# Attention output kept in columns: denominators beside every output row instead of transposes on TensorE

## The reference

```
Q, K, V = x @ Wq.T + bq, ctx @ Wk.T + bk, ctx @ Wv.T + bv      # split into 16 heads of 16
attn    = softmax(Q K^T / 4)                                   # (8, 16, 112, 375)
context = (attn V) joined back to (8, 112, 256)
y       = context @ W_o.T + b_o + x
out     = (y - mean(y)) / sqrt(var(y) + 1e-5) * gamma + beta
```

## Time and profile before

| | us |
|---|---|
| median of 3 runs | 141.18 |
| lowest, highest | 141.05, 143.31 |
| profiled execution | 142.0 |
| its span | 140.1 |
| TensorE busy | 129.5 (92%) |
| VectorE busy | 96.6 (69%) |
| ScalarE busy | 90.1 (64%) |
| GpSimd busy | 81.9 (58%) |

### The profile page before, as it was taken

One profiled execution on the slowest core, in us unless ns is written; L12 is line 12 of the kernel. 1 busy time (PEld: TensorE's weight loads), 2 busy tenths in 40 slices (PEclk: granted clock), 3 DMA queues, 4 the chain that ended last, 5 costly groups with the idle time before them and its releaser, 6 DMA issues.

```text
span 140.1 us, 3936 instructions
## 1 busy us (share of the span) xinstructions
PE 129.5 (92%) x1477; PEld 113.6 (81%) x1477; DVE 96.6 (69%) x225; ACT 90.1 (64%) x187; POOL 81.9 (58%) x105
## 2 busy tenths in 40 slices
PE   4999997699999999998999999999999999999960
PEld 4799965589788979797989998999899888878720
DVE  5987799787837883668559756975697787521442
ACT  0887545358476857767684959575957758788620
POOL 8358899991722852205279866850589007498271
PEclk9999999999999999999999999999999999999997
DMA  4997794875189942642235026732270100011102
GB/s 146 317 347 255 231 296 129 297 238 187 54 185 285 272 126 70 218 135 98 68 120 215 5 72 188 256 120 72 90 276 0 25 19 5 8 36 33 37 0 66
DMA packets 16099, 19.59 MB, mean 140 GB/s; under 512 B 2624, under 2 KB 15488, under 8 KB 16080
## 3 DMA queue, kind: packets, MB, share of 16 engines
q1 hardware_dynamic: 14960, 17.42, 38.4%
q0 software_dynamic: 640, 1.64, 4.8%
q10 hardware_dynamic: 480, 0.28, 0.7%
HBM read 6.30 MB, written 0.92 MB: 52 GB/s over the span
## 4 chain that ended last, share of the span: by engine, by line
PE 73%; SPq 9%; DVE 7%; DMA 5%; issue 3%; ACTq 1%; ACT 1%; POOLq 0%; DVEq 0%
PE m_bank L881 16%; PE pv_bank L993 14%; PE st_bank L975 14%; PE mx_bank L942 13%; PE m_bank L1025 4%; SPq L326 4%; SPq L266 4%; DMA q_stack<-shift_half 3%; PE m_bank L1004 2%; PE mx_bank L975 2%; DMA q_stack<-shift 2%; DVE k_stack L725 2%; DVE mx L748 2%; PE m_bank L902 1%; PE m_bank L1012 1%
## 5 line engine op out<-in xcount | busy, mean ns | idle before, releaser
L748 DVE TENSOR_REDUCE mx<-mx_bank 112x1 f32<-112x375 f32 x128 | 63.7, 541 | 22.3 <-PE mx_bank L942 21.9
L633 ACT ACTIVATE pw<-st_bank 125x448 f32<-125x448 f32 x86 | 45.1, 546 | 18.1 <-PE st_bank L975 17.8
L942 PE MATMUL mx_bank<-k_stack,q_stack 128*112 128x376 f32 x128 | 43.3, 352 | 0.2
L975 PE MATMUL st_bank<-q_stack,k_stack 128*125 128x224 f32 x172 | 34.9, 284 | 2.3 <-DMA q_stack<-shift_half 1.8
L975 PEld LDWEIGHTS st_bank<-q_stack,k_stack 128*125 128x125 f32 x172 | 28.5, 186 | 6.1 <-issue 3.6
L942 PEld LDWEIGHTS mx_bank<-k_stack,q_stack 128*112 128x112 f32 x128 | 22.0, 176 | 3.4 <-DVE mx L748 1.7
L430 POOL TENSOR_TENSOR k_hl<-k_full,k_hl 128x376 fp32r<-128x376 f32 x10 | 10.0, 1001 | 20.2 <-ACT k_hl L549 20.2
L993 PE MATMUL pv_bank<-pw,v_sb 125*17 125x112 f32 x744 | 21.5, 260 | 0.0
L993 PEld LDWEIGHTS pv_bank<-pw,v_sb 125*17 125x17 f32 x744 | 16.7, 97 | 3.1 <-issue 1.9
L881 PE MATMUL m_bank<-w_hl,c_hl 128*125 128x256 f32 x126 | 18.2, 282 | 0.0
L404 POOL TENSOR_TENSOR c_hl<-c_raw,c_hl 128x752 fp32r<-128x752 f32 x6 | 11.1, 1854 | 10.5 <-ACT c_hl L520 10.5
(11 more groups left out here) (113 smaller groups left out, 177.1 us busy)
## 6 DMA issues: line engine op xcount, KB each, us to landing
k_stack<-k_hl SPq DMA_DIRECT2D x48, 188.0 KB, 2.7
c_raw<-ctxT SPq DMA_DIRECT2D x7, 375.0 KB, 3.8
q_stack<-q_hl SPq DMA_DIRECT2D x9, 112.0 KB, 2.2
x_space<-x_nat SPq DMA_DIRECT2D x4, 224.0 KB, 3.2
out<-yo SPq DMA_DIRECT2D x8, 112.0 KB, 2.0
pw<-wT SPq DMA_DIRECT2D x2, 256.0 KB, 4.2
q_stack<-q_hl POOLq DMA_DIRECT2D x3, 168.0 KB, 2.8
q_stack<-q_hl SPq DMA_DIRECT2D x3, 168.0 KB, 2.8
```

The lines of the kernel that those rows point to most:

```text
L633: nc.scalar.activation(p_tile[0:KC, n % PR, :, :], st_of(n)[0:KC, 0:4 * Q].rearrange("p (j q) -> p j q", j=4), ACT.Exp, scale=float(DK) ** ...
L748: nc.vector.tensor_reduce(mx[b % 2][:, h % 2, q_pair(h // 2):q_pair(h // 2) + 1], mx_bank[n % MR][0:Q, 0:KV], axis=AX_X, op=ALU.max, negat ...
L942: nc.tensor.matmul(mx_bank[n % MR][0:Q, 0:KVP], q_stack[k][:, side, q_pair(h // 2), b - Q_STACKS[k][0], :], k_stack[b % 3][:, h // 2, :], ...
L975: last = nc.tensor.matmul(st_of(n)[0:KC, k * 2 * Q:(k + 1) * 2 * Q], k_stack[i % 3][:, 2 * g + k, c * KC:(c + 1) * KC], q_stack[qk][:, :, ...
```

## The change

V gets 32 columns a head instead of 17: between its 16 columns stand 16 of ones (`VW = 2 * DK`, `v_sb` is `[..., DK, 2]`). The product with the exponentials then has an output row and a row of its denominators in turn, on all 128 partitions. `wo` and the bias of V are put in the order of these rows on the host (`by_output`).

For batches 0 to 6 the transposes of the raw and of the scaled output are gone. ScalarE copies the bank three times: to `o_raw`, its first groups of each pair to `o_normT`, the second to `den` (for batch 6 VectorE does it). Two transfers then put the odd rows of `o_normT` and the even rows of `den` in place. VectorE inverts `den` whole, GpSimd multiplies and adds the bias in two halves. OUT and the layer norm run two batches behind instead of three, and for batch 6 in the last batch.

```diff
-VW = DK + 1
+VW = 2 * DK
-U_OUT, U_OT, U_Q, U_CONTEXT = 0, 6, 11, 5
+U_OUT, U_LN, U_Q, U_CONTEXT, U_NORM = 5, 7, 11, 5, 8
-NORM_WITH = {3: 0, 4: 1, 5: 2, 6: 3, 7: 5}
-U_MT = (8, 7, 6, 6, 6, 6, 5)
+U_MT = (8, 7, 7, 7, 7, 7, 4)
+OUT_AT = {i: U_OUT for i in range(2, B - 2)} | {B - 2: 8, B - 1: 5}
+NORM_AT = {i: U_LN for i in range(2, B - 2)} | {B - 2: 8, B - 1: 5}
...
+            def swap_rows(b):
+                sp.wait_ge(o_raw_ready, b + 1)
+                raw = o_raw[b % 2][:, :].rearrange("p (e s q) -> p e s q", e=EC, s=2)
+                sp.dma_start(den[0:PART - 1:2, :, :], raw[1:PART:2, :, 0, :]).then_inc(swap_in[b % 2], 16)
+                sp.dma_start(o_normT[b % 2][1:PART:2, :, :], raw[0:PART - 1:2, :, 1, :]).then_inc(swap_in[b % 2], 16)
...   # SyncE, in each batch i >= 1, after K's transfers and ahead of the next context and shift
+                if i >= 1:
+                    swap_rows(i - 1)
...   # GpSimd
+            nc.gpsimd.memset(v_sb[2][:, :, :, :, :], 1.0).then_inc(v_ones[2], 1)
+            def scale_output(b):
+                pool.wait_ge(rden_ready, b + 1)
+                nc.gpsimd.tensor_tensor(o_normT[b % 2][:, :, :], o_normT[b % 2][:, :, :], den[:, :, :],
+                                        op=ALU.mult).then_inc(o_scaled, 1)
+                pool.wait_ge(o_scaled, b + 1)
+                pool.wait_ge(bv_in, 16)
+                for e in range(EC):
+                    last = nc.gpsimd.tensor_scalar(o_normT[b % 2][:, e, :], o_normT[b % 2][:, e, :], bv[:, e:e + 1], None,
+                                                   op0=ALU.add)
+                last.then_inc(o_normT_ready, 1)
...
                 if i + AHEAD < B:
-                    for t in range(2):
-                        subtract_k(i + AHEAD, t)
+                    subtract_k(i + AHEAD, 0)
+                if i >= 1:
+                    scale_output(i - 1)
+                if i + AHEAD < B:
+                    subtract_k(i + AHEAD, 1)
...
             for b in range(B - V_AHEAD - 3, B - 1):
                 inverse_deviation(b)
                 scale_rows(b)
+                if b + 2 < B - 1:
+                    scale_output(b + 2)
             inverse_deviation(B - 1)
...   # ScalarE, units 1 and 2 of batches 1 to 6
+            nc.scalar.copy(v_sb[1][:, :, :, :, 1], v_sb[0][:, :, :, :, 1]).then_inc(v_ones[1], 1)
+            def take_raw(b):
+                act.wait_ge(pv_done, NG * (b + 1))
+                if b >= 2:
+                    act.wait_ge(swap_in[b % 2], 32 * (b // 2))
+                nc.scalar.copy(o_raw[b % 2][:, :], pv_bank[:, 0:NG * Q])
+            def take_o(b):
+                src = pv_bank[:, 0:NG * Q].rearrange("p (e s q) -> p e s q", e=EC, s=2)
+                if b >= 2:
+                    wait_full(act, "OUT", b - 2)
+                nc.scalar.copy(o_normT[b % 2][:, :, :], src[:, :, 0, :])
+                if b >= 1:
+                    act.wait_ge(o_scaled, b)
+                nc.scalar.copy(den[:, :, :], src[:, :, 1, :]).then_inc(o_raw_ready, 1)
-            def take_o_norm_t(b, *job):
...   # VectorE: units 2 and 4 of batch 7 for batch 6, unit 8 else
-            nc.vector.memset(v_sb[0][:, :, :, :], 1.0).then_inc(v_ones, 1)
-            nc.vector.memset(pv_bank[:, :], 0.0).then_inc(pv_clear, 1)
+            nc.vector.memset(v_sb[0][:, 0, :, :, :], 1.0).then_inc(warm_ready, 1)
+            nc.vector.memset(v_sb[0][:, 1:NC, :, :, :], 1.0).then_inc(v_ones[0], 1)
-            def normalise(b):
+            def take_o_last():
+                b = B - 2
...   # the same three copies on VectorE
+            def invert(b):
+                dve.wait_ge(swap_in[b % 2], 32 * (b // 2 + 1))
+                nc.vector.reciprocal(den[:, :, :], den[:, :, :]).then_inc(rden_ready, 1)
...   # TensorE
-            def transpose_o(b):
-            def norm_columns(dst, b):
-            def transpose_o_norm(b):
                     for h in heads[:1]:
                         scores_for_max(h)
+                    if i + 1 < B and u == U_MT[i]:
+                        transpose_max(i + 1)
+                    if i >= 2 and u == OUT_AT[i]:
+                        out_project(i - 2)
...
```

More of the change, by code:

```diff
@@ L72 @@
 for _i in range(1, B - V_AHEAD):
-    if _i >= 3:
-        M1_JOBS.append(("OUT", _i - 3))
     M0_JOBS.append(("V", _i + V_AHEAD, 0))
     M1_JOBS.append(("V", _i + V_AHEAD, 1))
-    M0_JOBS.append(("MT", _i + 1))
-    M1_JOBS.append(("OT", _i - 1))
+    if _i >= 2:
+        M0_JOBS.append(("OUT", _i - 2))
+    M1_JOBS.append(("MT", _i + 1))
     if _i + AHEAD < B:
@@ L128, in build @@
                 .rearrange("p (s e n) -> p s e n", s=2, e=EC))
-        v_sb = [sb(f"v_sb{i}", [PART, NC, H, VW]) for i in range(VR)]
+        v_sb = [sb(f"v_sb{i}", [PART, NC, H, DK, 2]) for i in range(VR)]
         ident = sb("ident", [PART, PART])
@@ L140, in build @@
         rden = sb("rden", [Q, H, 1])
-        o_norm = [sb(f"o_norm{i}", [Q, H, DK]) for i in range(2)]
+        o_norm = sb("o_norm", [Q, EC, 4, DK, 2])
+        den = sb("den", [PART, EC, Q])
         o_normT = [sb(f"o_normT{i}", [PART, EC, Q]) for i in range(2)]
@@ L174, in build @@
         ident_clear, ident_ready = sem("ident_clear"), sem("ident_ready")
-        pv_clear = sem("pv_clear")
         k_ones = [sem(f"k_ones{i}") for i in range(3)]
         q_clear = [sem(f"q_clear{k}") for k in range(NQ)]
-        v_ones = sem("v_ones")
+        warm_ready, v_ones = sem("warm_ready"), [sem(f"v_ones{i}") for i in range(VR)]
         m_full = [sem(f"m_full{i}") for i in range(len(JOBS))]
@@ L186, in build @@
         o_raw_ready, rden_ready = sem("o_raw_ready"), sem("rden_ready")
-        o_norm_ready, o_normT_ready = sem("o_norm_ready"), sem("o_normT_ready")
+        o_scaled, o_normT_ready = sem("o_scaled"), sem("o_normT_ready")
+        swap_in = [sem(f"swap_in{i}") for i in range(2)]
         xb_ready = sem("xb_ready")
@@ L229, in build @@
             "V": lambda b, n: (v_ready, 2 * b + n + 1),
[L230 to L233, removed]
+            "MT": lambda b, *half: (shift_ready, half[0] + 1 if b == 0 else b + 2),
             "OUT": lambda b: (z_ready, b + 1),
@@ L641, in _ @@
                             stack_shift_half(act, 1, part)
-                    if u == (1 if i < B - 1 else 2) and i >= 1:
+                    if u == 1 and 1 <= i < B - 1:
+                        take_raw(i - 1)
+                    if u == 2 and 1 <= i < B - 1:
                         take_o(i - 1)
@@ L738, in _ @@
             context_lo(1)
-            for i in range(1, VR):
-                nc.vector.memset(v_sb[i][:, :, :, DK:VW], 1.0).then_inc(v_ones, 1)
             for t in range(2):
@@ L1144, in by_stack, with by_output @@
     return a.reshape(2, 4, 2, DK, *rest).transpose(0, 2, 3, 1, *range(4, 4 + len(rest))).reshape(D, *rest)
+def by_output(a):
+    rest = a.shape[1:]
+    return a.reshape(EC, 2, 4, DK, *rest).transpose(0, 2, 3, 1, *range(4, 4 + len(rest))).reshape(D, *rest)
 def kernel(x, ctx_1024, L0_xattn_W_qkv, L0_xattn_b_qkv, L0_xattn_W_o, L0_xattn_b_o, L0_xattn_ln_gamma,
```

130 lines of the change are left out of this document (44 added, 86 removed).

## The result

The kernel after takes **147.03 us** (median of 4, 146.46 to 147.48), the kernel before on the same chip 141.28: ratio 1.0382, 95% interval 1.0329 to 1.0435. It is slower by 5.7 us, where 140.8 was forecast, and lies above the whole range of 137.0 to 143.7. The profiled execution took 147.48, with a span of 145.7, 5.6 more than before.

The account below looks back on a forecast made before the run. TensorE, 92% busy, was taken as the bound. Values of batch 6 would end at 125.32 - 4.8 + 0.5 = 121.0, OUT start 7.4 later at 128.4, GpSimd's queue end the span at 139.7: 140.8 us, range 137.0 to 143.7.

Parts of the forecast that it names:

- P at 121.0: Start to the end of batch 6's values (P): moves from 125.32 to 121.0, by 4.8 less and 0.5 added.
- I cost the queue at nothing: SyncE's queue, start to P: two more transfers a batch cost nothing; if late, a batch starts 1.2 late.
- 0.2 in all: VectorE's inversion of 128x224 before P: takes 1.35, costs TensorE at most 0.2 in some batches, 0.2 in all.
- Rival E: Inversion becomes VectorE's bound above some 1.9 us; maxima wait 0.7 in each of six batches, 4.2 back: 145.0; chance 0.13.
- the transposes' 0.7: TensorE's body up to P: removed transposes count in full, 2.2 for the raw and 1.0 for the normalised output.
- P to OUT, 7.4: From P to OUT of batch 6: a chain of four engines takes 7.35 to 7.4 instead of 4.9; OUT at 128.4.
- some 3: Between P and OUT of batch 6: TensorE stands still for some 3 us.
- TensorE's is unchanged: From OUT of batch 6 to the end: TensorE's path unchanged but for 0.3 at most, ending at 138.6.
- case A: The forecast: GpSimd's queue sets the end, 140.8, with 1.2 either side; chance 0.47.
- B: GpSimd's bias adds or inversion cheaper, or layer norms sooner; OUT's own chain sets the end: 139.7; chance 0.17.
- C: Chain from P to OUT so short that TensorE hardly waits; all transposes count, 4.8: 136.4; chance 0.11.
- D: Weight loads of 32 columns bind, 0.111 a round instead of 0.095, 2.7 more up to P: 143.5; chance 0.12.

Follow-up runs that it names:

- e8: The changed kernel with SyncE's six Q transfers for batches 6 and 7 issued ahead of the shift of batch 4: 146.07 us, ratio 1.0296.
- e4: The changed kernel with the inversion cut to 16 of the 224 elements of a partition, other denominators not inverted: 143.67 us, ratio 1.0095.
- e14: The changed kernel with batch 6 by transposes as before, Q's transfers early and the inversion cut as in e4: 140.22 us, ratio 0.9877.
- e13: The changed kernel with batch 6 by transposes, Q's transfers early, and batch 3's layer norm moved from batch 5 to unit 3 of batch 6: 141.16 us, ratio 0.9950.
- e16: e8 with OUT of batches 0 to 3 put back in the first unit of the batch three on: 145.37 us, ratio 1.0226.
- e1b: The changed kernel with eight unread filler products on TensorE ahead of OUT of batch 6, run again for its trace: 146.01 us, ratio 1.0290.
- e6: The kernel before with V's weights of 32 columns instead of 17 and nothing else of the change: 142.35 us, ratio 1.0042.
- e17: The changed kernel with OUT of batches 0 to 3 put back alone, Q's transfers as they were: 144.75 us, ratio 1.0199.
- e2: The changed kernel with the transposes of the maxima of batches 3 to 6 at unit 6 instead of 7: 146.99 us, ratio 1.0361.
- e5: The kernel before with TensorE's OUT of batch 6 made to wait for three VectorE memsets: 148.59 us, ratio 1.0463.

## Why the prediction was wrong

**P at 121.0.** This step failed, by 3.9 of the 6.0 in the span. Its removals were right as work, and the prices of the parts were near, but three terms that it covered by idle time, or put at nothing, were not covered.
- "I cost the queue at nothing": wrong by 1.4 in the profiled execution (e8). The K transfers stand behind the six Q issues of one batch, and in the kernel before there was 0.4 of slack. TensorE now comes 1.9 earlier to the product that needs them, K's issues only 1.3 earlier. This is worth 0.2 to 0.5 (e8), and the rest of the 1.4 is the slow landing, 4.86 instead of 4.0, whose cause is open.
- The inversion "0.2 in all": wrong by 1.1 to 1.2 in the second half of batch 5 (e4, e14). It took 1.55, not 1.35, which matters little; its place among the maxima does, and, as I read it, that TensorE has no projections to do meanwhile in this half. VectorE's idle time says nothing of that: with 0.8 of other work taken away TensorE waited the same 1.00 (e13). Rival E names the mechanism, but in six batches at 0.7 where it was one at 1.1, and below its own point of 1.9 us.
- The prediction moves OUT past the halves without pricing the place it leaves. It credits each batch with the transposes' 0.7, and batches 3 and 4 gave nothing: OUT left a half that ScalarE sets at 7.15 for one that TensorE sets (e16). The credit was 0.7 for each, and with Q early (e8) they came out 0.1 and 0.2 longer than before: 1.7 in all.

These come to 4.3, and batch 5 lost near 0.4 besides: OUT's 0.86 left its second half for the first, and the second is only 0.55 shorter than before even with the short inversion (5.00 for 5.55, e4). Against it stands an earlier start: values of batch 1 come 0.7 earlier after than before, though they differ as much between e8 and e16, so it may be the execution's.

**P to OUT, 7.4.** The chain of four engines is right and TensorE stood still 3.6, not "some 3". It measured 8.4. The copies were right (1.25), issue and landing took 3.5 instead of 2.85 (0.71 to the second issue, 2.75 behind it), the inversion 1.6 with its wait instead of 1.4, GpSimd 2.0 instead of 1.75. The landing is the term that was mis-sized: 2.2 was the median of another transfer. These take 1.9 in the median too, but 2.7 to 3.3 at this place in seven kernels.

**The tail.** "TensorE's is unchanged" failed. The prediction had an idle TensorE of 3 us in its own sum and priced the products behind it at full speed. The clock cost 1.4 against GpSimd's path (e1b). The Trainium skill (TensorE: Matmul & The Clock Gate, Part 1) has the two levels that the rows show, 1.00 and 0.50. The kernel before shows the fall as well, behind TensorE's last product, where it cost nothing:

```profile
138.00:140.10 2.10, 0.00 (x0) 0.00 (x0) 0.00 (x0) 0.00 (x0) 0.00 (x0) 0.52 0.19 55
```

GpSimd's path, case A, was right as a mechanism: it sets the end when the clock is held up (e1b). In the kernel after it did not.

**The rivals.** B and C did not come. D is refuted (e6). E was partly right. No rival had the clock or ScalarE's half, and with P 3.9 later the prediction's own sum would have given 144.7.

**Open.** Why the transfer of K that TensorE waits for takes 4.86 from its issue in the kernel after and 3.90 in e4, with one issue of 2.1 us behind it in the kernel after, is not settled; e17 changed it without touching SyncE. Nor is it settled what decides when the clock falls: TensorE stood still for 3.36 in e17 and OUT still took 1.09, for 3.45 in e2 and OUT took 2.02, for 2.79 in e4 and OUT took 1.55.

## What to carry over

Before an operation is moved, ask for the half-batch it leaves and the one it enters which engine sets each: time freed under another engine's pace is worth nothing (0.05 for OUT in a K half), and time added where TensorE leads costs all that the next engine's pace does not cover (0.53 of OUT's 0.86 in a V half). Read the cover from that very stretch, not from a mean batch; ask not only how long an engine is idle there but what stands before and behind the new operation in its queue. Look for the next transfer that arrives just in time. A change that leaves TensorE idle for some us has to be charged for the slow clock behind the gap as well, so for the last-but-one batch the transposes, between which TensorE has other work, beat the chain over four engines that leaves it idle.

## What was not expected of the hardware

- The reciprocal costs 6.3 ns an element at this length: 1546 ns for 224 elements a partition against 243 for 16. The slope from the short ones, 5, was too low.
- After gaps of 3.6, 3.9 (e16) and 5.2 us (e5) the four products of OUT took 2.0 us instead of 0.86, and in the kernel after the granted clock stayed at 0.50 through some 5 us of work. The length of the gap alone does not tell: after 2.79 (e4) the clock fell within OUT, after 3.36 (e17) only behind it.
- A row swap of 56 KB within the chip's own memory takes 1.9 us from issue to landing in the median and 2.75 at the end, in e16 3.11 and in e4 3.27.
